# A reciprocal over 1024 columns replaced by selecting both scales in the FP6 quantizer

## The reference

```python
scales = jnp.maximum(jnp.max(jnp.abs(blocks), axis=-1) / 7.5, eps)
q = _nearest_on_grid(blocks / scales[..., None], _GRID)   # ties go to the lower grid value
...
out = (xq * xs) @ (wq * ws).T + bias
```

## Time and profile before

| | us |
|---|---|
| median of 3 timed runs | 2057.77 (2057.50 to 2058.26) |
| the profiled execution | 2059.11 |
| span of its slowest core (core 7) | 2057.5 |
| spans of the 8 cores | 2051.0 to 2057.5 |
| VectorE busy | 1241.1 (60%) |
| TensorE busy (matmul) | 773.0 (38%) |
| ScalarE busy | 540.1 (26%) |
| granted TensorE clock, mean | 0.724 of full speed |

### The profile page before, as it was taken

The page is one execution under the profiler, slowest core; times in us unless marked ns, Lnnn a source line. Parts: engine busy times, 40 slices in busy tenths (PEclk is TensorE's granted clock), DMA queues, the critical chain, the costliest instruction groups (busy, mean ns, idle before and its releaser), DMA issues.

```text
span 2057.5 us, 15307 instructions; the slowest of 8 cores (2051.0 to 2057.5 us)
## 1 busy us (share of the span) xinstructions
PE 773.0 (38%) x3776; PEld 354.9 (17%) x3776; DVE 1241.1 (60%) x1485; ACT 540.1 (26%) x1414; POOL 20.8 (1%) x41
## 2 busy tenths in 40 slices
PE   0010013222234047595695545555455022322332
PEld 0000001111111023242242222223222011111110
DVE  0499889999997123241104555555522599999992
ACT  3411121111111740001234444444303411222110
POOL 0000000000000010000000000000000000000000
PEclk9999995556556558797897666667678565556556
DMA  6000010000000045433100000000053000000004
GB/s 195 21 20 21 0 41 0 0 0 0 0 0 0 24 163 182 151 135 102 62 0 1 1 1 1 1 1 1 8 157 123 0 0 0 0 0 1 0 1 163
DMA packets 18852, 81.26 MB, mean 39 GB/s; under 512 B 2000, under 2 KB 2000, under 8 KB 16464
## 3 DMA queue, kind: packets, MB, share of 16 engines
q1 hardware_dynamic: 11904, 53.02, 7.9%
q0 software_dynamic: 6864, 27.27, 3.8%
HBM read 61.41 MB, written 18.87 MB: 39 GB/s over the span
## 4 chain that ended last, share of the span: by engine, by line
DVE 48%; PE 25%; ACT 10%; issue 8%; DMA 5%; DVEq 1%; SPq 1%; ACTq 0%; POOL 0%; POOLq 0%
DVE arena L60 48%; PE psc L60 19%; ACT arena L60 10%; PE pbig L60 4%; PE pt L60 2%; DVEq L68 1%; DMA arena<-wo 1%; DMA arena<-wk 1%; DMA arena<-wq 1%; DMA arena<-wv 1%; DMA arena<-ident 1%; SPq L60 1%; DMA arena<-wg 1%; ACTq L68 0%; POOL out L60 0%
## 5 line engine op out<-in xcount | busy, mean ns | idle before, releaser
L60 PE MATMUL psc<-arena 128*128 128x512 bf16 x2112 | 589.6, 435 | 137.2 <-DVE arena L60 116.1
L60 PE MATMUL pt<-arena 128*128 128x128 bf16 x576 | 134.0, 264 | 1111.9 <-ACT arena L60 623.6
L60 DVE TENSOR_TENSOR arena<-arena 128x1024 f32<-128x1024 f32 (+3 forms) x347 | 285.6, 823 | 36.9 <-DVE arena L60 0.9
L60 DVE TENSOR_SCALAR arena<-arena 128x1024 f32<-128x1024 f32 (+4 forms) x308 | 142.0, 483 | 269.1 <-ACT arena L60 188.2
L60 PEld LDWEIGHTS psc<-arena 128*128 128x128 bf16 x2112 | 221.9, 108 | 431.6 <-issue 271.6
L60 DVE RECIPROCAL arena<-arena 128x1024 f32<-128x1024 f32 (+2 forms) x99 | 280.2, 2831 | 10.7 <-DVE arena L60 0.7
L60 ACT ACTIVATE arena<-arena 128x1024 f32<-128x1024 f32 (+2 forms) x187 | 184.2, 986 | 362.8 <-DVE arena L60 354.3
L60 PEld LDWEIGHTS pt<-arena 128*128 128x128 bf16 x576 | 60.3, 105 | 1194.6 <-issue 1183.5
L60 DVE SCALAR_TENSOR_TENSOR arena<-arena 128x1024 f32<-128x1024 int32 (+3 forms) x171 | 191.3, 1119 | 21.3 <-DVE arena L60 6.6
L60 DVE TENSOR_TENSOR arena<-psc,arena 128x128 bf16<-128x128 f32 (+1 forms) x192 | 81.0, 424 | 176.4 <-PE psc L60 160.7
L60 ACT COPY arena<-pt 128x128 bf16<-128x128 bf16 x576 | 135.0, 266 | 195.9 <-PE pt L60 194.9
(11 more groups left out here) (13 smaller groups left out, 106.5 us busy)
## 6 DMA issues: line engine op xcount, KB each, us to landing
arena<-x SPq DMA_DIRECT2D x4, 2048.0 KB, 19.4
xspill<-arena POOLq DMA_DIRECT2D x16, 512.0 KB, 3.1
arena<-qsc SPq DMA_DIRECT2D x8, 1024.0 KB, 5.9
arena<-ksc SPq DMA_DIRECT2D x8, 1024.0 KB, 5.7
arena<-xspill POOLq DMA_DIRECT2D x16, 512.0 KB, 3.9
out<-arena POOLq DMA_DIRECT2D x4, 2048.0 KB, 16.4
arena<-wf SPq DMA_DIRECT2D x8, 512.0 KB, 3.4
arena<-wq SPq DMA_DIRECT2D x8, 512.0 KB, 4.1
```

The costliest lines, as they stand in the source:

```text
L60: inst = getattr(getattr(self.nc, eng), name)(*a, **k)
```

## The change

Only `q_B1` is changed. Before, it selected r by two comparisons (qb1 >= 4, qb1 >= 16) scaled by -4 and -2 and added to 8; multiplied y by r; and computed 1/r with a reciprocal over the whole tile. Now the two comparisons are scaled by 1/8 and 1/4 and added to 1/8, which gives 1/r (1/8, 1/4 or 1/2) in `qb2` directly. r is then formed in `rb_buf` by two more instructions: rb = 24 rb + 12, then rb = -32 qb2 + rb, which gives 8, 4 or 2. y is multiplied by `rb_buf`. The reciprocal and the wait behind it are gone, and the function ends with the multiplication.

```diff
         def q_B1(p, yy_s):
             c.wait("vector", "s", yy_s)
-            c.op("vector", "tensor_scalar", qb2, qb1, 4.0, -4.0,
+            c.op("vector", "tensor_scalar", qb2, qb1, 4.0, 0.125,
                  ALU.is_ge, ALU.mult).inc("v")
-            c.op("vector", "tensor_scalar", rb_buf, qb1, 16.0, -2.0,
+            c.op("vector", "tensor_scalar", rb_buf, qb1, 16.0, 0.25,
                  ALU.is_ge, ALU.mult).inc("v")
             c.wait("vector", "v")
-            c.op("vector", "scalar_tensor_tensor", qb2, qb2, 8.0, rb_buf,
+            c.op("vector", "scalar_tensor_tensor", qb2, qb2, 0.125, rb_buf,
                  ALU.add, ALU.add).inc("v")
             c.wait("vector", "v")
-            c.op("vector", "tensor_tensor", qby_y[p], qby_y[p], qb2,
+            c.op("vector", "tensor_scalar", rb_buf, rb_buf, 24.0, 12.0,
+                 ALU.mult, ALU.add).inc("v")
+            c.wait("vector", "v")
+            c.op("vector", "scalar_tensor_tensor", rb_buf, qb2, -32.0, rb_buf,
+                 ALU.mult, ALU.add).inc("v")
+            c.wait("vector", "v")
+            c.op("vector", "tensor_tensor", qby_y[p], qby_y[p], rb_buf,
                  ALU.mult).inc("v")
-            tq_v = c.cnt["v"]
-            c.wait("vector", "v")
-            c.vsync(c.op("vector", "reciprocal", qb2, qb2))
-            return tq_v
+            return c.cnt["v"]
```

## The result

The changed kernel takes 1866.27 us (median of 10 runs; the kernel before 2057.84 us, median of 10). The ratio is 0.9079, 95% interval 0.9059 to 0.9098; it is that of the means, which one run of 1884.88 us pulls up, and the medians alone give 0.9069. The forecast was 1872, the range 1863 to 1892. The profiled execution has a span of 1866.3 us against 2057.5: 191.2 us less, where the sum said 185.7.

A forecast was written before the change was run, and what follows sets the result against it. VectorE was taken to bound the three quantizing loops. Savings of 177.6 + 3.6 + 5.8 - 1.3 = 185.7 us took the profiled 2059.1 to 1873.4; timed runs lie 1.3 lower, so 1872 us, range 1863 to 1892.

The forecast's parts named there:

- VectorE bounds the three loops, and the reciprocal is on its path: In the three quantizing loops VectorE sets the time; an interior tile goes from 8.06 to 3.26 us, 4.80 saved.
- The added instructions: In q_B1, the scalar operation in place was taken at 0.80 us with its gap, the second scalar-tensor-tensor at 1.32.
- Rival B: In q_B1 the new scalar operation misses the faster pace, 1.33 us with gap: 21 us more, 1893 us; chance 0.05.
- No wait behind the product: At q_B1's end the next reduce starts 1.14 us after the product, with 1.32 as the bound.
- Rival C: Behind q_B1's product the missing wait saves nothing: 6.7 us less saved, 1879 us; chance 0.06.
- What the cover hid: From T, ScalarE's cast start: q_B2 at 3.70 us, burst at 5.42, evacuation at 11.75; bursts over 6.15 us are late.
- The term of 1.3 us for late bursts: Inside the x loops, one in four of 28 evacuations waits 0.2 us for TensorE's burst, 1.3 us lost.
- Rival A: In the x loops all bursts run at the lower clock and delay each evacuation: 20 us lost, 1891 us; chance 0.07.
- D: TensorE becomes the bound of the x loops, evacuations waiting for bursts: slower, about 2086 us just past break-even; chance 0.01.
- The loop ends: The last tile of each x loop saves 5.0 us less 2.1 ahead of ScalarE's cast: 2.9, twice 5.8 us.
- The other 942 us: LN, projections, retention, output projection and statistics: forecast difference 0, with 4 us allowed either way for drift.

The follow-up runs named there:

- exponent_bits: The changed kernel with q_B1 shortened by one two-input pass, both scales written as exponent bits by scalar operations with integer output: 1818.13 us, ratio 0.8834.
- keep_wait: The changed kernel with one line more, VectorE waiting for its own product before the next reduce: 1876.34 us, ratio 0.9115.
- half_burst: The changed kernel with 8 instead of 16 matmuls per tile in the x loops: 1865.91 us, ratio 0.9066.
- merged_b2: The kernel of exponent_bits with q_B2 in five passes instead of seven, the comparison inside scalar-tensor-tensor: 1785.2 us, ratio 0.8675.

## Why the prediction was right, step by step

*VectorE bounds the three loops, and the reciprocal is on its path.* Shown: without it each tile is 4.79 us shorter in the timeline (25.18 to 20.39), and with it put back 4.80 + 2.12 a tile come back.

*The added instructions.* The scalar operation 0.69 us and 0.80 to its follower, the sum 1.33: both at the prices taken from the earlier trace rows. Rival B is out, in this kernel and, with integer output, in exponent_bits.

*No wait behind the product.* 1.14 us as taken. Rival C is out. The bound I had set for it, 1.32, was too low: in the row that it came from the wait for VectorE's own result is the last one in front, here ScalarE's wait would stand behind it, and keep_wait shows 1.40. A nearer case was on show: the first pass of `q_B2`, which also has a wait behind that for VectorE's own result, starts 0.17 us after its forerunner's end (355.96 + 1.28 to 357.42 here, the same before).

*What the cover hid.* The distances to T (3.7 for `q_B2`, 11.75 for the evacuation, 5.4 for the burst) came out to the hundredth. The term of 1.3 us for late bursts was too large for core 2, whose span is the measured one: no evacuation inside its loops shows a wait. (As worked it should have been 1.4: seven waits of 0.2 us.) Its bursts there took 5.0 to 6.1 us, and the one of 6.26 started earlier, in an iteration without `x_d`. But this is near to luck. The tightest iteration of the second loop, T = 1775.94:

```profile
1781.36 6.12 PE L60 MATMUL psc<-arena 128*128 128x512 bf16 x16 [0.61 <-ACT arena L60]
...
1787.70 1.23 DVE L60 SCALAR_TENSOR_TENSOR arena<-psc,arena 128x1024 f32<-128x1024 f32 x1
```

The burst ends at 1787.48, and with the handoff of 0.18 there are 0.04 us to spare, where the iteration shown further up had 0.6. On core 7 of the same execution, which is not the slowest, the first loop has the late burst that the prediction described:

```profile
256.29 6.47 PE L60 MATMUL psc<-arena 128*128 128x512 bf16 x16 [0.50 <-ACT arena L60]
...
262.93 1.23 DVE L60 SCALAR_TENSOR_TENSOR arena<-psc,arena 128x1024 f32<-128x1024 f32 x1 [0.37 <-PE psc L60]
```

Beyond the usual 0.10 us its evacuations inside the loops wait 1.1 us in all, those of cores 4 and 0 wait 0.4 and 0.2, those of the other five none. So the mechanism of the term is shown and its size was right for one core of eight.

Rival A is out: in half_burst nothing is given back, and the bursts inside the loops took 5.0 to 6.5 us, not 6.9. In the Trainium skill, page "TensorE: Matmul & The Clock Gate", section "HAM oscillation — how this bites in real kernels", the bursts that start cold are of about 2 us. I had drawn the full 20 us from it; these bursts are two to three times as long and get faster inside, so it did not speak for the full price.

The mechanism of D is real, as the two runs with the early evacuation show, and needs the evacuation in another place; merged_b2, which brings it 1.4 us nearer, pays it.

*The loop ends.* This term was sized too small: 5.8 us forecast. From T to the last evacuation it was 25.0 and 24.0 us before, and is 18.9 and 16.4 now, so 4.0 and 5.4 us are gained after the 2.1 ahead of T, 9.4 in all. What the sum had left unchanged there was the last burst's length: it went from 6.42 to 5.08 and from 5.40 to 3.61 us. Faster last bursts stood in the prediction's range only, with about 3 us, and the excess is 3.6. In which loop of which core the last burst runs at the upper level throughout was not foreseen.

*The other 942 us.* They were taken as unchanged and are 2.0 us shorter between these two cores. Projections of 256 matmuls still take 57 to 58 us. From the start of the last input projection to that of the output projection, by the starts of their matmuls, the slowest core took 488.1 us before (core 7) and 486.8 after (core 2), so 1.3 of the 2.0 us lie in this stretch, which is mostly retention. It differs by core and not clearly by the change: core 2 took 486.4 before and 486.8 after, core 7 488.1 and 482.5, core 0 486.1 and 484.5. What sets it was not tried; the 4 us of drift that the prediction allowed held it.

Of the 5.5 us by which the sum was short in the profiled spans, 3.6 are the loop ends, 1.3 the waits that did not come, 2.0 the later stages; the weight loop (0.6) and the ends outside (0.5) go the other way. The rest is under half a microsecond.

## What to carry to other kernels

Before an instruction is taken off a busy engine, write down what the other engines do from its start on, and when the next instructions of its own engine want their results: the gain is the instruction's length up to the first such result that is not yet there. In this kernel it came within 0.04 us of costing something on the slowest core and did cost up to 1.1 us on others, and the same change with one other order of calls gained 11 us instead of 191. Instructions added ahead of the point that releases the other engines cost their full price even when the removed one cost nothing; and once a wait shows up, part of what is saved by shortening the work ahead of it goes into the wait (29 of 56 us here), and moving the waiting call to where its data has long been ready gets that back (27 us).

## What the runs showed of the hardware

- A reciprocal over 128 x 1024 float32 takes 6.55 us on VectorE, over five times a two-input operation (1.23) and nine times a scalar one (0.69).
- From a two-input operation of this shape to the next instruction pass 1.14 us behind an already met wait on another engine, 1.33 behind a wait for its own result, and 1.40 where a met wait on another engine stands behind that one.
- TensorE's bursts of 16 matmuls after a pause of 8 us and more begin at the 1.2 GHz level and get faster within the burst (4.8 to 6.5 us instead of 6.9). Cut to 8 matmuls they stay at the lower level (3.44 us), nearly as long as a full burst at the upper level (3.61 us).
- The last burst of an x loop of the changed kernel, which follows the one ahead at about 3 us, ran at the upper level throughout (3.61 us) in the ten loop ends where the burst ahead took 4.9 to 6.1 us, and took 5.0 to 5.15 us in the six where that took 6.16 to 6.42. Why the two go together was not tried.
